# A fused FFN, Mamba and FFN block: the second pass puts one row's FFN units a slot later and one gate product into another slot

## The reference

```
def ffn(x, weight, bias):              # weight rounded to -1, 0, 1 times its mean absolute value
    scale = mean(abs(weight)); w_t = clip(round(weight / scale), -1, 1)
    return x @ (w_t * scale).T + bias
def mamba(x):
    u, z = split(x @ W_in.T)           # 1024 channels each
    u = silu(conv_b + causal_conv4(u, conv_w))
    dt_r, Bm, Cm = split(u @ W_xproj.T)            # 64, 16, 16
    dt = softplus(dt_r @ W_dt.T + b_dt); A = -exp(A_log)
    h_t = exp(dt_t * A) * h_(t-1) + dt_t * Bm_t * u_t     # 16 states for each channel
    y_t = sum over states of h_t * C_t
    return ((y + u * Dskip) * silu(z)) @ W_out.T
x = x + 0.5 * ffn(LN(x)); x = x + mamba(LN(x)); out = x + 0.5 * ffn(LN(x))
```

## Time and profile before

| what | value |
|---|---|
| runs | 2957.45, 2961.16, 3604.93 us; median 2961.16 |
| span of the profiled execution | 2958.3 us, 37688 instructions; the page gives no other time of this execution |
| second pass | from about 1085 us to the end |
| busy share of the span | PE 82%, DVE 80%, ACT 68%, POOL 63% |
| mean granted TensorE clock | 0.911 of full speed |

### The profile page before, as it was taken

One profiled execution on the slowest core, in us unless ns is written; L12 is line 12 of the kernel. 1 busy time (PEld: TensorE's weight loads), 2 busy tenths in 40 slices (PEclk: granted clock), 3 DMA queues, 4 the chain that ended last, 5 costly groups with the idle time before them and its releaser, 6 DMA issues.

```text
span 2958.3 us, 37688 instructions
## 1 busy us (share of the span) xinstructions
PE 2439.5 (82%) x12448; PEld 1400.3 (47%) x12448; DVE 2378.5 (80%) x3197; ACT 2024.5 (68%) x3520; POOL 1874.5 (63%) x1673
## 2 busy tenths in 40 slices
PE   3577998998998736788888888888888889888897
PEld 1233444444443315555555555555555555555553
DVE  5566667677666649999999999999999999999992
ACT  2233766666766767778777777778777777777783
POOL 1112222222221138989989989989989989899991
PEclk8778999999999857889989999999989999999999
DMA  6454233233332256675675775676666766766744
GB/s 206 165 199 165 92 129 121 94 129 114 101 129 105 82 201 157 150 175 123 168 179 115 171 172 124 168 169 131 170 160 133 172 149 150 168 140 157 170 98 100
DMA packets 200290, 429.26 MB, mean 145 GB/s; under 512 B 44512, under 2 KB 93920, under 8 KB 199840
## 3 DMA queue, kind: packets, MB, share of 16 engines
q1 hardware_dynamic: 160928, 284.23, 29.1%
q0 software_dynamic: 39168, 142.62, 25.5%
HBM read 190.86 MB, written 110.10 MB: 102 GB/s over the span
## 4 chain that ended last, share of the span: by engine, by line
DVE 36%; PE 9%; ACT 7%; issue 6%; POOL 4%; DMA 1%; SPq 0%; DVEq 0%; POOLq 0%; ACTq 0%
DVE h L1268 25%; DVE y L1281 7%; PE p_g L1406 4%; POOL dbu L1064 3%; ACT p_da L1156 3%; PE p_ht L1372 2%; ACT tokt L1186 1%; ACT tokt L1193 1%; DVE x L1305 1%; PE p_g L1389 1%; ACT y_part L1173 1%; DVE q L1294 1%; DVE small L55 1%; DVE o L1315 1%; PE p_g L1415 1%
## 5 line engine op out<-in xcount | busy, mean ns | idle before, releaser
L1268 DVE TENSOR_TENSOR_SCAN h<-p_da,dbu 128x512 f32<-128x512 f32 x1024 | 1187.8, 1206 | 135.5 <-ACT p_da L1156 110.6
L1064 POOL TENSOR_TENSOR dbu<-dtu_,bb 128x1024 f32<-128x1024 f32 x512 | 1231.8, 2494 | 21.5 <-DMA dtu_<-dtu_scratch 20.9
L1156 ACT ACTIVATE p_da<-dt_,neg_a 128x255 f32<-128x255 f32 x2048 | 882.1, 467 | 331.8 <-DVE h L1268 325.9
L1372 PE MATMUL p_ht<-ident,h 128*128 128x128 f32 x4096 | 575.0, 300 | 131.5 <-DVE h L1268 128.6
L1372 PEld LDWEIGHTS p_ht<-ident,h 128*128 128x128 f32 x4096 | 520.6, 156 | 220.5 <-DVE h L1268 197.3
L714 PE MATMUL p_u<-xz,wu 128*128 128x512 f16 x1536 | 349.2, 385 | 8.2 <-DVE xz L508 6.2
L1406 PE MATMUL p_g<-wo,tokt 128*128 128x512 f16 x1536 | 350.7, 386 | 1.6 <-ACT tokt L1193 1.6
L1281 DVE SCALAR_TENSOR_TENSOR y<-p_ht,ct,y 128x1024 f32<-128x1024 f32 x272 | 344.3, 1266 | 8.0 <-PE p_ht L1372 7.7
L1415 PE MATMUL p_g<-wz,xz 128*128 128x512 f16 x1536 | 346.4, 382 | 0.0
L70 POOL TENSOR_TENSOR small<-small,consts 128x1 f32<-128x1 f32 x96 | 68.8, 717 | 423.9 <-DVE small L63 423.9
L363 POOL TENSOR_TENSOR late<-dt,u 128x512 f32<-128x512 f32 x64 | 81.6, 1274 | 376.9 <-DVE dt L561 376.9
(11 more groups left out here) (117 smaller groups left out, 2862.0 us busy)
## 6 DMA issues: line engine op xcount, KB each, us to landing
y<-y_part POOLq DMA_DIRECT2D x224, 512.0 KB, 5.8
bb<-b_scratch SPq DMA_DIRECT2D x128, 256.0 KB, 3.6
xin<-in_x SPq DMA_DIRECT2D x32, 512.0 KB, 5.8
x_scratch<-x SPq DMA_DIRECT2D x32, 512.0 KB, 5.1
xz_scratch<-xz SPq DMA_DIRECT2D x16, 1024.0 KB, 6.2
y_scratch<-late SPq DMA_DIRECT2D x32, 512.0 KB, 5.4
dt_scratch<-dt SPq DMA_DIRECT2D x64, 256.0 KB, 2.1
dtu_scratch<-late SPq DMA_DIRECT2D x64, 256.0 KB, 2.4
```

Source lines behind the costliest of these rows:

```text
L1064: nc.gpsimd.tensor_tensor(state[:, 4 * f:4 * f + 4, :], dtu[:, 4 * f:4 * f + 4, :], bb[n // NB % 2][:, n % NB:n % NB + 1, :].to_broadcast( ...
L1156: ins_ = nc.scalar.activation(p_da[p % 2][:, k * T2 + 1:(k + 1) * T2], dt[:, g, 1:], ACT.Exp, scale=neg_a[:, g, n:n + 1])
L1268: nc.vector.tensor_tensor_scan(h[n % 2][:, 2 * p:2 * p + 2, :].rearrange("p g t -> p (g t)"), p_da[p % 2][:], dbu[n % 2][:, 2 * p:2 * p + ...
L1372: mm = nc.tensor.transpose(p_ht[t][:, g * P:(g + 1) * P], h[n % 2][:, g, t * P:(t + 1) * P], ident[:])
```

## The change

Row 1's "n" units move from slot 15 of body i - 1 to slot 0 of body i, its "f" units from slots 0 and 1 to slots 1 and 2. The gate product of row 0, half 1 moves from slot 3 to slot 15 of the same body, that of row 0, half 0 from slot 2 to slot 3. What belongs to them follows: `take_high` and `low` of row 1 from slot 0 to 1, `high` from slot 15 to slot 0, `finish` from slots 1 and 2 to 2 and 3, the two stores by one slot, tanh and `silu_part` of half 0 from slot 3 to 4, those of half 1 from slot 4 to slot 0 of the next body, and `load_xz` from slot 14 to the end of slot 15, behind the loads of dt. `base`, `place` and `Z_NTH` keep the bank counts right.

```diff
-        FFN = {0: [("f", 1, 0)], 1: [("f", 1, 1)]}
+        FFN = {0: [("n", 1, 0), ("n", 1, 1)], 1: [("f", 1, 0)], 2: [("f", 1, 1)]}
         OUT = {4: [("t", 0, 0), ("t", 0, 1)], 5: [("o", 0, 0)], 6: [("o", 0, 1)], 7: [("t", 1, 0), ("t", 1, 1)],
                8: [("o", 1, 0)], 9: [("o", 1, 1)], 10: [("n", 0, 0), ("n", 0, 1)], 13: [("f", 0, 0)],
-               14: [("f", 0, 1)], 15: [("n", 1, 0), ("n", 1, 1)]}
-        ZED = {2: [("z", 0, 0)], 3: [("z", 0, 1)], 11: [("z", 1, 0)], 12: [("z", 1, 1)]}
+               14: [("f", 0, 1)]}
+        ZED = {3: [("z", 0, 0)], 11: [("z", 1, 0)], 12: [("z", 1, 1)], 15: [("z", 0, 1)]}
+        Z_NTH = {(0, 0): 0, (1, 0): 1, (1, 1): 2, (0, 1): 3}
...
-                     (flags(i)[1] and n == 11, i, "n", 0), (flags(i)[0] and n == 0, i - 1, "n", 1)) if on]
+                     (flags(i)[1] and n == 11, i, "n", 0), (flags(i)[0] and n == 1, i - 1, "n", 1)) if on]
...
-            return (i - 2) * 10 + 11
+            return (i - 2) * 10 + 10
...
+            j = i + 1 if (kind, t) == ("n", 1) else i
...
# SyncE
-                        b, m = place(c - 1, "z", 1, 1)
+                        b, m = place(c - 1, "z", 0, 1)
...
-                        if e_on and n in (1, 2, 3):
-                            store(i - 2, *{1: (0, 1), 2: (1, 0), 3: (1, 1)}[n])
+                        if e_on and n in (1, 3, 4):
+                            store(i - 2, *{1: (0, 1), 3: (1, 0), 4: (1, 1)}[n])
...
-                        if z_on and more(i) and n == 14:
+                        if z_on and more(i) and n == 15:
                             load_xz(i + 1)
...
# ScalarE
-                        if z_on and n in (3, 4, 12, 13):
-                            tanh(i, n // 12, n - 3 if n < 12 else n - 12)
+                        if c_on and n == 0:
+                            tanh(c, 0, 1)
+                        if z_on and n in (4, 12, 13):
+                            tanh(i, n // 12, n - 12 if n >= 12 else 0)
...
+                        if e_on and n == 0:
+                            high(i - 1, "n", 1)
...
-                            if n in (10, 15):
-                                high(i, "n", n // 15)
+                            if n == 10:
+                                high(i, "n", 0)
...
# VectorE
-                            if n in (3, 4, 12, 13):
-                                silu_part(i, n // 12, n - 3 if n < 12 else n - 12)
+                        if c_on and n == 0:
+                            silu_part(i - 1, 0, 1)
+                        if z_on and n in (4, 12, 13):
+                            silu_part(i, n // 12, n - 12 if n >= 12 else 0)
...
-                        if e_on and n in (1, 2):
-                            finish(i, i - 2, 1, n - 1)
+                        if e_on and n in (2, 3):
+                            finish(i, i - 2, 1, n - 2)
```

More of the change, by code:

```diff
@@ L900, in base @@
                 return base(C2) + 8
-            return (i - 2) * 10 + 11
+            return (i - 2) * 10 + 10
         def place(i, kind, t, x):
-            at = [u[1:] for u in sequence(i)].index((kind, t, x))
-            return at % 2, base(i) + at // 2
+            j = i + 1 if (kind, t) == ("n", 1) else i
+            at = [u[1:] for u in sequence(j)].index((kind, t, x))
+            return at % 2, base(j) + at // 2
         def more(i):
@@ L1292, in silu_part @@
                     b, m = place(i, "z", t, x)
-                    wait(dve, th_done, i * 4 + 2 * t + x + 1)
+                    wait(dve, th_done, i * 4 + Z_NTH[t, x] + 1)
                     nc.vector.scalar_tensor_tensor(out=q[2 * t + x][:], in0=q[2 * t + x][:], scalar=1.0, in1=p_g[b][:],
@@ L1375, in unit @@
                 def unit(i, par, kind, t, x):
-                    b, m = place(i, kind, t, x)
+                    b, m = place(i - 1 if (kind, t) == ("n", 1) else i, kind, t, x)
                     wait(pe, g_free[b], m)
@@ L1385, in unit @@
                             src = xn
-                            wait(pe, xn_done, (i - 1) * TT2 + t + 1)
+                            wait(pe, xn_done, (i - 1 - t) * TT2 + t + 1)
                         for k in range(4):
```

## The result

The changed kernel takes 3018.22 us (median of 4 runs, 3015.78 to 3019.91), the kernel before, on the same chip, 2962.88. The ratio is **1.0193**, 95% interval 1.0178 to 1.0209: slower by 1.9%. (One run of the kernel before, 3604.93 us, was disturbed and is not in the ratio.) The profiled execution took 3017.58 us, its span 3015.8 us at a mean granted clock of 0.904.

A forecast was written before the change was run, and what follows sets the result against it. No engine full; DVE waits for ACT's exponentials, 3.99 us ahead of slot 0. A gain of 0.6 against a loss of 1.3, taken as 0.3 lost, times 15 bodies is 4.5 us on 2958.3: 2963 us, range 2940 to 2992.

The forecast's parts named there:

- the price of the B rows: B rows for states 2 and 3, behind xz in SP's queue, wanted by POOL at 2224.1: cost 0 to 0.8 us.
- most of xz ahead of the accumulations: SP's transfers had the engines nearly alone up to 2219, so a loss of 0.3 us a body was taken.
- The rival of a late load: POOL waits ahead of slot 2's product or at the merge: 20 us (2978) to 38 us (2996); chance 0.20.
- The accumulation of state 14: POOL's merge waits for it; landing at 2233.7 behind all of xz costs 1.3 us, at 2232.3 behind half, nothing.
- the whole rule: Engines alternate between queues and completion follows earlier writes from any queue: accumulation pays 1.3 us a body, 2978 us in all.
- The gain of DVE's side: Slots 0 to 3: one output half moves to slot 3, so DVE starts slot 3 0.6 us earlier.
- 0, give or take 1: Effect at the kernel's end, after the last scan, where the chain through the last FFN units is the same.
- dt: Its first quarter lands at 2216.5, so 1.5 of slot 0's 4.0 us wait can go, leaving 2 to 2.6.
- The sign of being wrong that was named for POOL: The prediction is wrong if POOL runs slots 0 to 3 in other than 21 to 23 us.
- The new wait ahead of slot 1: DVE waits for ACT, whose work there matches slots 4 and 5 before the change: 0.86 us, about 0.9.
- POOL as the next bound: POOL's slot 3 product ends 0.1 us before DVE takes it; POOL limits the chunk's gain to 1.0 us.
- The clock: Around the body's end it stays near 1.0 with the gate product in PE's gap; worth 0.

The follow-up runs named there:

- the one with B first: The changed kernel with the B rows of states 2 and 3 sent before xz in slot 15; 2967.98 us, ratio 1.0019.
- the one without xz: The changed kernel without loads of xz for chunks 1 to 15, all gate products using chunk 0's xz; 2957.93 us, ratio 0.9986.
- x1 out of the way: The changed kernel with B rows sent ahead of xz, and x1's row 0 loaded in slot 4 instead of slot 1; 2960.52 us, ratio 0.9995.
- the kernel without it: The changed kernel without loads of xz and of dt after the first chunk's; 2941.62 us, ratio 0.9930.

## Why the prediction was wrong

**The step that failed is the price of the B rows**: "Cost 0 to 0.8" a body. It measured 4.2 as POOL's wait (63.4 us in 15 times) and 3.3 as time (the 50.2 us between the changed kernel and the one with B first, over 15). Of that step two parts came out. POOL's product of slot 0 ends 34.0 us later in the changed trace than in the one before (2249.59 and 2215.58); on the scale of before, xz is sent at 2215.4 (forecast 2215.3), B at 2216.3 (2216.1), and POOL wants B at 2224.2 (2224.1). The landing time was wrong: 5.9 and 2.9 for xz make 8.8 us, 11.7 were measured. The 2.9 came from the rate of a stretch in which SP's queue had 98% of the engines. That rate held to 2254, about four microseconds after B was sent. From there SP's queue got 0.31, 0.20 and 0.15 MB in 2 us. The choice of "most of xz ahead of the accumulations" overlooked that B stands behind xz in SP's queue and then moves at the shared rate. The kernel before already had that rate on view: at 2212 to 2214, with dt's loads under way, its two queues stand at 77% and 25%, and SP's moves 0.17 MB; I read the stretch next to it.

**The rival of a late load** named place and mechanism rightly, and was still too small: 2.5 us a body against 3.7. The landing that it took at worst, 2227.6, is close to the 2228.0 measured (on the scale of before), but it was borrowed from the slowest transfer of the other queue, so that is luck. The rest is POOL's path from slot 0 to slot 3, 3.1 us longer than before, and waits for PE, below.

**The accumulation of state 14** was priced at a loss of 1.3 us a body at most, and of 0.3 by choice. The kernel with B first, in which only this wait is left, is 10 us above the one without xz, 0.7 a body, and its merge waits 18.7 us. Against the kernel before it is 4.8 us slower, and with the 3.1 that its end gains that makes about 0.5 a body. With x1 out of the way it is 2.6 us above the one without xz, 0.2 a body. That bytes ahead of it in another queue hold up a completion agrees with the rule of the Trainium skill quoted in the prediction (DMA: Bandwidth & Descriptors, Queues, rings and completion order); that they do so for the reason given there no run shows. With the whole rule the loss against the kernel before would be 1.3 a body; it was less than half.

**The gain of DVE's side**, 0.6 us a body, did not come. The kernel without xz loads has it in the chunk at 2218.03 and not in the mean of 14 bodies, 112.69 us against 112.74: the waits of slots 0 and 1 together are 3.93 in that chunk where 3.99 stood. What the units' move gives lies in part at the end, 3.1 us where the prediction had "0, give or take 1".

**What held.** *dt*: forecast to end the wait at 2 to 2.6 us; 2.42 measured, with the dt load as releaser (51.4 us in 17 times), and the kernel without it confirms it. The sign of being wrong that was named for POOL, slots 0 to 3 in other than 21 to 23 us, came true with 25.66. *The new wait ahead of slot 1*: 0.86 forecast, 1.15 measured. *POOL as the next bound*: seen ahead of slot 2 with dt gone. *The clock*: 1.00 at 2245 to 2250 of the changed kernel, as forecast, and worth nothing there, as the row of that stretch shows (length, then busy time of PE, PEld, DVE, ACT and POOL, granted clock, DMA share, GB/s):

```profile
2245.00:2250.00 5.00, 5.00 (x29) 2.69 (x28) 4.14 (x5) 1.91 (x3) 3.23 (x4) 1.00 1.02 257
...
2290.00:2294.00 4.00, 4.00 (x16) 2.88 (x16) 4.00 (x4) 3.16 (x7) 4.00 (x4) 0.50 0.55 148
```

PE is busy throughout, DVE still waits for dt. The second row belongs to what stays open: later in the body the clock falls to 0.50, after PE had waited 1.06, 1.19 and 0.50 us from 2284 on, and the W_out product of 24 matmuls takes 6.38 us, the next one at 1.00 5.34. DVE waits 0.63 and 0.86 us for PE's turns at 2299.69 and 2306.97, where it waited 0.34 before. Those 1.15 us more, less the 0.42 that slots 0 and 1 gave back, are about the 0.6 us between the body's 3.7 and POOL's 3.1. It was not tested by itself. The kernel without xz loads has one such wait, 0.76 us, in its body, so a part of it belongs to the moved units.

**The sum by measured terms**: the units' move -5.2 (kernel without xz, 3.1 of it at the end), the bytes of xz ahead of the accumulation and the rest +10.0, the B rows behind xz +50.2. Together 55.

## What to carry to other kernels

Price a load that moves into a full stretch by what stands behind it in its own queue, and at the rate that this queue gets while the other one runs, not while it is alone; the cure that worked here is to send what is wanted first ahead of it. A wait that several things would end within two microseconds of each other is worth at most the distance to the second of them, here 1.6 of the 4.0 us that looked to be had, and the work that moves can fill that too: over 14 bodies 0.05 us a body was left. Compare many chunks before a gain of half a microsecond is believed; one chunk here showed 0.6. In a queue that issues in order, a load that waits for a product delays every load behind it.

## What the runs showed of the hardware

While both queues had work, the packets came out nearly even: in each of the six stretches of 1 us from 2255 to 2261 of the changed kernel, SP's queue has 36 to 48 packets and POOL's 35 to 48. But the shares do not. In 2258 to 2260 a packet of POOL's queue took 0.295 us (83.1% of 16 engines for 2 us, over 90), one of SP's 0.084 (23.1%, over 88). The first carried 3.7 KB in the mean, the second 1.7, so a part of the difference is size and a part is time for each KB, 0.080 us against 0.049. In those six stretches SP's queue had 22 to 35% of the engines and POOL's 72 to 84%. The Trainium skill (DMA: Bandwidth & Descriptors, Queues, rings and completion order) says that an engine goes round its queues packet by packet; the even counts agree.
